# First seven node tiles of a graph layer made inside the edge stage, and the node stage begun at the eighth

## The chip, the cores and the metric

One core of one Trainium2 chip runs the whole kernel as one program. The metric is the device time of that core in microseconds (us). Its engines are TensorE (PE, with its weight loads as PEld), VectorE (DVE), ScalarE (ACT), GpSimd (POOL) and SyncE (SP). SP issues plain transfers. POOL issues the indirect ones, the gathers and scatters by a list of row numbers.

## What is computed

The reference is a graph attention layer over 6,250 nodes and 200,000 edges (sorted by destination), and after it a mixture of 8 experts with 2 chosen for each node. Cut to what matters:

```python
enh = LN(x) + 0.1 * query_emb
Q, K, V = enh @ Wq + bq, enh @ Wk + bk, enh @ Wv + bv        # 4 heads of 64
scores = einsum(Q[dst], K[src] + 0.2 * rel_w[edge_type]) / 8
w = softmax of scores over the edges of each dst
agg = segment_sum(w * V[src], dst)                            # V itself where a node has no edge
x1 = x + LN(agg @ Wo + bo + LN(x)) * gamma + beta
logits = LN-input x1 @ Wr + br; two best experts, softmax weights
out = x1 + sum over the two: weight * (gelu(LN_e(x1) @ W1[e] + b1[e]) @ W2[e] + b2[e])
```

(The router reads the normalized x1, as the experts do.)

## The kernel before

Three stages follow each other: `prepare` (K and V of all nodes to DRAM, index tables), `edge_pass` (attention over the edges) and `finish` (node tiles, routing and experts).

**Edge stage.** The edges are cut into 261 groups (`NG`), each of 6 x 128 edges (`TG`), half of them from each of two streams that run through the sorted list side by side. Every engine runs `pipeline(...)`: steps up to `WARM` = 8 are written out, the rest is a loop on the chip of 6 steps a round (`U` = `RING` = 6), and the last two or three steps are written out again. A step of group g does this. POOL issues six indirect gathers of K and V rows (line 260), ahead by the ring of six buffers: it waits until group g-6 has been summed (`s_agg`). PE turns the K half of group g+1 (L502), makes the scores of g in `psD` (L523, L525, L531), sums group g-1 (L555, L544) and turns the weights of g (L578). DVE takes the row maximum of `psD` (L426), ACT the exponential (L353). SP stores finished sums (L234) and loads edge features (L242) once in three groups. In the first eight groups PE also makes pieces of Q ("units", L488), which ACT evicts (L315). POOL computes `spots`, the row of the sums that belongs to each node, after its last gather (L276 to L291).

**Last stage.** `finish` goes through 72 steps written out in full. Of the 49 tiles of 128 nodes (`NT`) one begins in each step. For tile t: SP loads V and x rows (L1507, L1508), POOL gathers its sums (L1579), DVE divides them (L1802 to L1809), PE turns the messages and multiplies by Wo (L2072, L2084, L2086), DVE and ACT normalize twice (L1818 to L1841, L1648, L1734, L1719), SP stores x1 to `out` (L1545), PE makes the logits (L2102). Seven tiles (`RN`) are a batch. Batch k is routed in three steps: the two best experts are picked (16 DVE operations, `R_AT`), slots are counted (17, `S_AT`), and the list of expert blocks is made (23, `T_AT`). Then ACT scales the rows and POOL scatters them to `d_xs` (L1655, L1625), 14 scatters a batch. Expert blocks of 128 rows (105 of them) start at step `START` = 15; the first seven come one a step, the others two a step. The first needs batch 0 scattered and listed. Before `START` the steps hold node tiles alone. SP also loads the expert weights W2 in eight pieces of 1 MB (L1539), at steps 2, 4, 5, 7, 8, 10, 11 and 13, and the first three of W1, 1 MB each (L1514), at step 13. The router weights, gamma, beta and the router bias are loaded at the start of the stage (L1521 to L1525), and the first tile's normalization waits for all five.

`hold` is a wait on a semaphore ahead of a DMA, and stands in every queue as one instruction (L94). Each engine and SP is one queue in program order.

Of the kernel before, what the change touches and what calls it, by code (L numbers as in the profile page):

```python
# [17 lines left out]
P = 128  # L18
# [5 lines left out]
W = 16  # L24
# [20 lines left out]
SPOTS = NG * P // 4  # L45
# [22 lines left out]
def pipeline(eng, n, lo, hi, unroll, warm, step):  # L68
# [70 lines left out]

RING = 6  # L140
# [7 lines left out]
def edge_pass(nc, ctx, cst, idx, QT, kv_dram, idxall, feat_dram, accs_dram, bases, delta, penc, relT, reach, keys, spots, wq, bqc):  # L148
# [24 lines left out]
    place = sb("e_place", [P, 8, NT])  # L173
# [8 lines left out]
    psL = ctx.enter_context(nc.psum_tensor("psL", [P, DC, QH], F32))  # L182
    MX, MC, MM, NM, AL, SUM = (slice(i, i + 1) for i in range(6))
# [4 lines left out]
    s_idx = sem("es_idx")  # L188
    s_rows = [sem(f"es_rows{i}") for i in range(U // HB)]
# [34 lines left out]
    with nc.Block() as blk:  # L224
        @blk.sync
        def _(sp):
# [19 lines left out]
            pipeline(sp, NHB, 0, 3, U // HB, 5, step)  # L246
# [4 lines left out]
        def _(pool):  # L251
# [12 lines left out]
            pipeline(pool, NG, 0, 0, U, WARM, step)  # L264
# [8 lines left out]
            def spotted():  # L273
# [15 lines left out]
                link(pool.tensor_scalar(last, last, float(-P // 4 - SPOTS), None, ALU.add))  # L289
                link(pool.tensor_tensor(row, last, kept, ALU.mult))  # L290
                link(pool.tensor_scalar(spots[:, :], row, float(SPOTS), None, ALU.add))  # L291
# [4 lines left out]
        def _(act):  # L296
# [83 lines left out]
            pipeline(act, NG, -AHEAD, HI, U, WARM, step)  # L380

        @blk.vector
        def _(dve):
# [8 lines left out]
            dve.wait_ge(s_init, 4)  # L392

            def step(T):
# [61 lines left out]
                if isinstance(g.t, int):  # L456
                    tile = g.t if 0 <= g.t < SOON else None
                else:
                    tile = g.rnd + (SOON - WARM // U) if g.slot == WARM % U else None
                if tile is not None:  # L460
# [6 lines left out]
            pipeline(dve, NG, LO, HI, U, WARM, step)  # L467

        @blk.tensor
        def _(pe):  # L470
# [111 lines left out]
            pipeline(pe, NG, LO, HI, U, WARM, step)  # L582
# [22 lines left out]
def prepare(nc, ctx, cst, io, out, dram, idx, QT, idxall, bases, delta, penc, relT, unfit, reach, keys, wq, wo, bqc, consts,  # L605
# [42 lines left out]
    early = sb("p_early", [1, 4])  # L648
# [53 lines left out]
    with nc.Block() as blk:  # L702
# [40 lines left out]
        def _(pool):  # L743
# [76 lines left out]
            pool.dma_start(dram["accs"][NG * P:].rearrange("(p a) x -> p (a x)", a=2), zero[0:P // 4, 0:2 * ROW]  # L820
# [35 lines left out]
        def _(dve):  # L856
# [18 lines left out]
            def setup():  # L875
# [94 lines left out]
                link(dve.tensor_copy(early[:, 3:4], misfits[0:1, 1:2]))  # L970
                yield
# [339 lines left out]
START = RN + 8  # L1311
# [33 lines left out]
assert all(step_of(b) >= (batch_of(b) + 1) * RN + 8 for b in range(NB))  # L1345


def finish(nc, ctx, cst, io, out, dram, rows, ints, spots, wo, lnst, biaso):


    def sb(name, shape, dt=F32):
# [909 lines left out]
```

## Time and profile before

| what | us |
|---|---|
| median of 3 runs | 3764.64 (3761.67 to 3767.57) |
| the profiled execution, its own time | 3765.22 |
| its span from first to last instruction | 3763.4 |
| edge stage, first to last score maximum (L426) | 172.9 to 2718.6 |
| last stage, first instruction to first expert matmul (L2133) | 2727.3 to 2843.9 |

The profile is one execution. A PE record shows when a matmul was handed to the array; its end is modelled. "<-" names what ended an idle time, "remote" is an event that the profile ties to no instruction, "issue" an idle time with no visible cause. In the windows view each engine has its busy time and, in brackets, its number of instructions; PEclk is the granted TensorE clock as a share of full speed.

### The profile page before, as it was taken

To read this page: it belongs to the slowest core of one execution; us is meant where nothing else is said; L and a number is where in the kernel's file an instruction comes from. 1 tells how busy PE (TensorE), PEld (TensorE's weight loads), DVE (VectorE), ACT (ScalarE), POOL (GpSimd) and SP (SyncE) were. 2 spreads that over 40 slices of the span, in tenths; PEclk is the share of its full clock that TensorE was granted. 3 is DMA by queue.
4 is the path that set the end of the run, shared out by engine and by line. 5 is a ranking of instruction groups with operands and counts; after the bars stand their busy time and mean duration, and the time that the engine had idled before them with its cause. 6 is when DMAs were issued, how large, how long until landed. Compare 5 with 4: busy or idle time off the path is not lost. (4 is left out here: it accounts for less than half of the span.)

```text
span 3763.4 us, 77621 instructions
## 1 busy us (share of the span) xinstructions
PE 2924.2 (78%) x21213; PEld 2095.5 (56%) x21213; DVE 1675.9 (45%) x6070; ACT 1452.9 (39%) x4666; POOL 1904.0 (51%) x2003
## 2 busy tenths in 40 slices
PE   8687777777777777777777777777757999999998
PEld 7454444444444444444444444444446888889898
DVE  7244444444444444444444444444476554563222
ACT  5343333333333333333333333333335655564332
POOL 6355555555555555555555555555434434432322
PEclk9898888888888888888888888888858999999999
DMA  7566666666666666666666666666476666666665
GB/s 230 165 171 191 184 187 184 190 189 187 184 184 188 189 188 184 187 184 191 188 183 187 184 191 189 185 187 184 138 232 191 200 199 195 197 182 184 188 183 133
DMA packets 295467, 701.49 MB, mean 186 GB/s; under 512 B 47432, under 2 KB 143071, under 8 KB 295188
## 3 DMA queue, kind: packets, MB, share of 16 engines
q0 software_dynamic: 151104, 456.15, 43.5%
q1 hardware_dynamic: 144212, 243.57, 21.2%
q8 instruction: 65, 1.06, 0.1%
q14 instruction: 86, 0.70, 0.1%
HBM read 633.18 MB, written 66.36 MB: 186 GB/s over the span
## 5 line engine op out<-in xcount | busy, mean ns | idle before, releaser
L260 POOL DMA_INDIRECT e_kv<-d_kv,idx x1566 | 1486.4, 949 | 1140.2 <-PE psA L544 690.3
L426 DVE TENSOR_REDUCE e_small<-psD 128x1 f32<-128x384 f32 x261 | 145.5, 557 | 1255.8 <-remote 1250.6
L502 PE MATMUL psK<-consts,e_kv 128*128 128x128 f32 x3132 | 604.3, 316 | 90.8 <-issue 84.2
L353 ACT ACTIVATE e_prob<-psD,e_small 128x384 f32<-128x384 f32 x261 | 151.5, 580 | 1321.4 <-DVE e_small L432 1309.8
L544 PE MATMUL psA<-e_kv,e_probT 128*32 128x128 f32 x6264 | 441.2, 290 | 219.8 <-issue 218.6
L502 PEld LDWEIGHTS psK<-consts,e_kv 128*128 128x128 f32 x3132 | 432.2, 162 | 143.0 <-issue 137.9
L578 PE MATMUL psP<-consts,e_prob 128*128 128x128 f32 x783 | 177.2, 346 | 349.5 <-ACT e_prob L353 349.5
L1600 POOL DMA_INDIRECT out<-f_y,f_whose x105 | 165.8, 1579 | 554.1 <-DVE f_y L1978 387.8
L2146 PE MATMUL f_psY<-f_w,f_hT 128*128 x1680 | 395.1, 389 | 40.0 <-ACT f_hT L1668 34.0
L544 PEld LDWEIGHTS psA<-e_kv,e_probT 128*32 128x32 f32 x6264 | 181.3, 110 | 429.1 <-issue 401.6
L2133 PE MATMUL f_psH<-f_xT,f_w 128*128 128x128 f32 x3360 | 404.3, 280 | 0.9 <-DVE f_xT L1966 0.9
L1668 ACT ACTIVATE f_hT<-f_psH,f_b 128x128 f32<-128x128 f32 x840 | 239.0, 369 | 419.2 <-PE f_psH L2133 343.9
L2133 PEld LDWEIGHTS f_psH<-f_xT,f_w 128*128 128x128 f32 x3360 | 396.6, 196 | 3.6 <-issue 1.3
L2146 PEld LDWEIGHTS f_psY<-f_w,f_hT 128*128 128x128 f32 x1680 | 317.3, 194 | 85.4 <-issue 45.6
L332 ACT COPY e_qb<-QT 64x32 f32 x1044 | 229.2, 220 | 276.4 <-issue 257.3
L578 PEld LDWEIGHTS psP<-consts,e_prob 128*128 128x128 f32 x783 | 98.7, 166 | 421.9 <-ACT e_prob L353 420.2
L399 DVE COPY e_kT<-psK 128x384 f32<-128x384 f32 x522 | 289.9, 555 | 92.8 <-remote 35.5
L531 PE MATMUL psD<-e_kT,e_qb 128*32 128x384 f32 x2088 | 297.2, 651 | 0.0
L338 ACT COPY e_kT<-psK 128x384 f32<-128x384 f32 x522 | 246.4, 472 | 32.8 <-remote 13.9
L555 PEld LDWEIGHTS psA<-e_accs,e_carry 128*128 128x128 f32 x522 | 93.4, 224 | 226.8 <-issue 225.8
L1966 DVE TENSOR_SCALAR f_xT<-f_psT,f_ln 128x128 f32<-128x128 f32 x210 | 76.7, 406 | 292.0 <-PE f_psT L2123 218.2
L525 PE MATMUL psD<-e_relhot,e_qrel_high 128*128 128x384 f32 x261 | 172.2, 660 | 0.0
(309 smaller groups left out, 4108.3 us busy)
## 6 DMA issues: line engine op xcount, KB each, us to landing
f_w<-in_W SPq DMA_DIRECT2D x113, 1024.0 KB
e_rows<-d_feat SPq DMA_DIRECT2D x174, 288.0 KB
e_kv<-d_kv,idx POOLq DMA_INDIRECT x1566
d_accs<-e_accs SPq DMA_DIRECT2D x348, 48.8 KB
f_xs<-d_xs SPq DMA_DIRECT2D x105, 132.5 KB
d_kv<-p_kv SPq DMA_DIRECT2D x48, 256.0 KB, 2.1
p_x<-in_x SPq DMA_DIRECT2D x49, 128.0 KB, 2.8
n_v<-d_kv SPq DMA_DIRECT2D x49, 128.0 KB
```

Of the source, the lines that this page charges most:

```text
L260: pool.indirect_dma_start(out=kv[g.slot][:, t, :], out_offset=None, in_=kv_dram[:, :], in_offset=bass.IndirectOffsetOnAxis(ap=idx[g.slot][ ...
L332: act.copy(qb[a.slot % R][o * HD:(o + 1) * HD, :].rearrange("p (c b w o) -> p c b w o", c=2, b=DC, o=2)[:, c, :, :, o], QT[o * HD:(o + 1) ...
L338: act.copy(kT[a.slot % 2][:, 1, j * GH:(j + 1) * GH], psK[:, 1, 0:GH]).then_inc(s_kTa, 1)
L399: dve.tensor_copy(kT[a.slot % 2][:, 0, j * GH:(j + 1) * GH], psK[:, 0, 0:GH]).then_inc(s_kTv, 1)
L502: mm = pe.transpose(psK[:, half, t * P:(t + 1) * P], kv[a.slot][:, third * TS + t, half * P:(half + 1) * P], ident)
L525: pe.matmul(scores, part[:, :], relhot[g.slot % R][:, :], start=False, stop=False)
L531: mm = pe.matmul(psD[own, g.slot % 2, 0:GH], qb[g.slot % R][:, own], kT[g.slot % 2][:, b, c * GH:(c + 1) * GH], start=False, stop=True, ti ...
L544: mm = pe.matmul(psA[own, 0:2 * HD], probT[c.slot % R][:, j, own], kv[c.slot][:, s * TS + j, D + b * P:D + (b + 1) * P], start=j == 0, sto ...
L578: mm = pe.transpose(psP[:, j * P:(j + 1) * P], prob[g.slot % R][:, j * P:(j + 1) * P], ident)
L1668: act.activation(hT[:, f, :], psH[:, f // FB % 2, f % FB * BK:(f % FB + 1) * BK], ACT.Gelu, bias=b1[:, bass.ds(e * FC + f, 1)]).then_inc(s ...
L2133: mm = pe.matmul(psH[:, f // FB % 2, f % FB * BK:(f % FB + 1) * BK], w1[g % RW][:, a, f * P:(f + 1) * P], xT[g % 2][:, a, :], start=a == 0 ...
L2146: mm = pe.matmul(psY[:, 0:D], hT[:, f, :], w2[:, bass.ds(e * (FC * D) + f * D, D)], start=f == 0, stop=f == FC - 1)
```

## The change

Seven of the 49 tiles (`FORE` = 7) are made inside the edge stage, one in every nine groups (`PACE`) from group 192 on (`FOREAT`), each spread over 12 groups with one short piece for an engine in a group. For this the loop on the chip ends at `UNTIL` = 183 and steps 182 to 262 are written out on every engine. The gathers of the seven tiles read only sums stored before group 180 (`STORED`); a check of the data sends everything to the slow path when that isn't enough. The row numbers of the seven tiles are worked out on DVE in groups 184 to 191 (16 operations, two a group), and POOL waits for them ahead of its first such gather. The constants for the tiles are loaded by SP in the edge stage. The last stage then has 42 tiles (`NTF`), its `START` is 8, batch 0 is picked in step 0, placed in step 1 and listed in step 2. It fetches the seven stored x1 tiles back and normalizes them in step 0. W2 is loaded at steps 1, 3, 4, 6, 7, 8, 9 and 10, each but the first behind a hold for the piece before, and the first seven expert blocks wait only for their own expert's piece. W1's first three pieces go to steps 4, 5 and 6.

The constants, the end of the loop, and which tile has its piece in a step:

```diff
-START = RN + 8
+START = RN + 8 - FORE
...
+FORE = RN
+PACE, HOPS = 9, 11
+FOREAT = (NG - 4 - PACE * (FORE - 1) - HOPS) // HB * HB
+STORED = FOREAT - 4 * HB
...
+    if until is not None:
+        loops = min(loops, (until - warm) // unroll)
...
+def fore_of(step, hop):
+    if not isinstance(step, int):
+        return None
+    j, past = divmod(step - FOREAT - hop, PACE)
+    return j if past == 0 and 0 <= j < FORE else None
```

At the end of an engine's edge step the piece for its hop follows: PE `turn` at hop 2, `project` 3, `turn_again` 9, `route` 10; DVE `summed` 1, `normed` 4, `attended` 6, `factor` 8, `routed` 10; ACT `first_norm` 1, `copied` 2, `spread` 5, `spread_again` 7, `second_norm` 8, `copied_again` 9; POOL `gather` 1 behind its six gathers; SP `load` 6 and `store` 12 in its feature step, which runs some five groups ahead of PE. Hop 10 of a tile is hop 1 of the next. The pieces hold the same operations as a tile has in `finish`, on one set of buffers. POOL's piece, and the ones that the prediction prices:

```diff
+                j = fore_of(g.t, 1)
+                if j is not None:
+                    if j == 0:
+                        pool.wait_ge(s_soon, SITES)
+                        for i in range(U // HB):
+                            hold(pool, s_out[i], 2 * DC * 16 * len(range(i, STORED // HB, U // HB)))
+                    fore.gather(pool, j, accs_all[0:P // 2 + STORED * P], soon)
...
+    def load(self, sp, j):
+        if j + self.runs:
+            hold(sp, self.s_st, self.moved(j, 16))
+            hold(sp, self.s_act, self.shaped(j - 1, self.H2))
+        sp.dma_start(self.v, self.kv[j * P:(j + 1) * P, D:2 * D]).then_inc(self.s_in, 16)
+        sp.dma_start(self.x, self.io["x"][j * P:(j + 1) * P, :]).then_inc(self.s_in, 16)
...
+    def gather(self, pool, j, table, spots):
+        if j + self.runs:
+            hold(pool, self.s_row, self.row(j - 1, self.SUM))
+        pool.indirect_dma_start(
+            out=self.agg, out_offset=None, in_=table.rearrange("(q a) x -> q (a x)", a=4),
+            in_offset=bass.IndirectOffsetOnAxis(ap=spots[:, j:j + 1], axis=0)).then_inc(self.s_ag, 16)
...
+    def spread(self, act, j):
+        act.preload_act_table(ACT.Sqrt)
+        act.wait_ge(self.s_row, self.row(j, self.NORM))
+        act.activation(self.st[:, 8:9], self.st[:, 7:8], ACT.Sqrt, bias=self.cst("eps")).then_inc(self.s_act, 1)
+        act.preload_act_table(ACT.Exp)
...
+    def turn(self, pe, j):
+        pe.wait_ge(self.s_row, self.row(j, self.SUM))
+        if j + self.runs:
+            pe.wait_ge(self.s_act, self.shaped(j, 0))
+        for b in range(DC):
+            mm = pe.transpose(self.ps[:, b * P:(b + 1) * P], self.msg[:, b * P:(b + 1) * P], self.cst("ident"))
+        mm.then_inc(self.s_mm, 1)
+
+    def project(self, pe, j):
+        pe.wait_ge(self.s_act, self.shaped(j, self.TURNED))
+        to = self.ps[:, D:2 * D]
+        pe.matmul(to, self.cst("ones")[0:1, :], self.biaso[0:1, :], start=True, stop=False)
+        for b in range(DC):
+            mm = pe.matmul(to, self.turned[:, b, :], self.wo[:, b, :], start=False, stop=b == DC - 1)
+        mm.then_inc(self.s_mm, 1)
```

In `finish`:

```diff
-    W2_AT = {2 + (3 * e + 1) // 2: e for e in range(NX)}
+    W2_AT = {s: e for e, s in enumerate((1, 3, 4, 6, 7, 8, 9, 10))}
...
+    picked_at = lambda s: 0 if s == 0 else batch(s, R_AT)
+    placed_at = lambda s: 0 if s == 1 else batch(s, S_AT)
+    listed_at = lambda s: 0 if s == 2 else batch(s, T_AT)
...
-            for a in range(DC):
-                sp.dma_start(wr[:, a, :], io["Wr"][a * P:(a + 1) * P, :]).then_inc(s_w, 16)
-            for j, name in enumerate(("gamma", "beta")):
...
             load(2)
+            for j in range(FORE):
+                sp.dma_start(h2[j][:, :], out[j * P:(j + 1) * P, :]).then_inc(s_rows, 16)
             load(3)
...
+                    if e:
+                        hold(sp, s_w2, e * 16)
...
+                if s == 0:
+                    act.wait_ge(s_set, SETS)
+                    for j in range(FORE):
+                        act.wait_ge(s_rows, 16 * FORE)
+                        act.activation(h2[j][:, :], h2[j][:, :], ACT.Identity, bias=nb[:, j:j + 1], scale=rs[:, j:j + 1]
+                                       ).then_inc(s_fore, 1)
...
-                if c == 0:
+                if c < certain(0):
+                    pe.wait_ge(s_w2, (e + 1) * 16)
+                elif c == certain(0):
                     pe.wait_ge(s_w2, 16 * NX)
```

## Rows read from the trace of the kernel before

**Rows 1.** Windows: us, busy of PE, PEld, DVE, ACT, POOL, PEclk, DMA share, GB/s.

```profile
172.00:239.00 67.00, 60.32 (x423) 43.70 (x424) 32.92 (x105) 32.37 (x100) 28.69 (x30) 0.94 0.49 135
...
600.00:1600.00 1000.00, 728.17 (x5701) 446.48 (x5699) 426.17 (x1557) 343.26 (x1219) 578.70 (x611) 0.85 0.66 187
...
2703.00:2718.00 15.00, 15.00 (x162) 9.43 (x162) 10.77 (x43) 9.99 (x31) 0.84 (x3) 1.00 0.06 13
2727.00:2744.00 17.00, 7.14 (x18) 4.26 (x18) 9.02 (x32) 3.42 (x7) 8.92 (x13) 0.50 0.73 206
2744.00:2786.00 42.00, 29.73 (x100) 21.43 (x99) 35.64 (x129) 18.39 (x49) 11.46 (x18) 0.58 0.87 285
2786.00:2844.00 58.00, 25.74 (x85) 18.31 (x83) 36.44 (x154) 20.91 (x55) 22.87 (x27) 0.56 0.67 218
2844.00:2930.00 86.00, 73.35 (x448) 67.39 (x449) 60.45 (x209) 53.88 (x123) 35.74 (x38) 0.91 0.54 164
```

**Rows 2.** One line's instructions (L426, one a group) in three stretches.

```profile
L426 DVE TENSOR_REDUCE e_small<-psD x7: 548/558/558, 172.9 to 239.3; 128x1 f32<-128x384 f32 x7
L426 DVE TENSOR_REDUCE e_small<-psD x102: 556/557/559, 300.6 to 1293.7; 128x1 f32<-128x384 f32 x102
L426 DVE TENSOR_REDUCE e_small<-psD x4: 557/558/559, 2703.3 to 2718.6; 128x1 f32<-128x384 f32 x4
```

**Rows 3.** Waits, 1000 to 2000 us: total, times, longest.

```profile
DVE e_small L426 <- remote: 502.0, 101, 6.3
POOL e_kv L260 <- PE psA L544: 268.1, 102, 3.2
```

**Rows 4.** Timeline of one group late in the edge stage: start, us.

```profile
2670.67 0.94 POOL L260 DMA_INDIRECT e_kv<-d_kv,idx  x1 [2.65 <-PE psA L544]
...
2674.18 1.51 PE L531 MATMUL psD<-e_kT,e_qb 128*32 128x384 f32 x8
...
2676.92 0.95 POOL L260 DMA_INDIRECT e_kv<-d_kv,idx  x1 [0.30 <-issue]
...
2679.26 0.56 DVE L426 TENSOR_REDUCE e_small<-psD 128x1 f32<-128x384 f32 x1 [5.00 <-remote]
```

**Rows 5.** Timeline of an early group.

```profile
220.29 0.94 POOL L260 DMA_INDIRECT e_kv<-d_kv,idx  x1 [2.96 <-PE psA L544]
...
228.81 0.56 DVE L426 TENSOR_REDUCE e_small<-psD 128x1 f32<-128x384 f32 x1 [4.85 <-remote]
```

**Rows 6.** L488, the extra units of the first groups: ns min/median/max.

```profile
L488 PE MATMUL psL<-QT,wq x112: 377/379/747, 175.6 to 238.7; 128*128 128x256 f32 x112
```

**Rows 7.** L1822 (one a tile) in two stretches, and L2133 from its first.

```profile
L1822 DVE TENSOR_TENSOR n_xb<-n_x,n_vec x9: 424/426/427, 2743.7 to 2785.6; 128x256 f32<-128x256 f32 x9
L1822 DVE TENSOR_TENSOR n_xb<-n_x,n_vec x7: 424/424/426, 2785.6 to 2836.8; 128x256 f32<-128x256 f32 x7
L2133 PE MATMUL f_psH<-f_xT,f_w x234: 274/275/554, 2843.9 to 2930.0; 128*128 128x128 f32 x117
```

**Rows 8.** Timeline of the first tiles of the last stage.

```profile
2733.51 0.69 PE L2072 MATMUL n_psM<-consts,n_msg 128*128 128x128 f32 x2 [5.01 <-DVE n_msg L1809]
...
2734.98 2.08 PE L2086 MATMUL n_psO<-wo,n_turned 128*128 128x256 f32 x4
...
2741.02 0.42 DVE L1818 TENSOR_TENSOR n_y<-n_psO,n_xn 128x256 f32<-128x256 f32 x1 [4.40 <-DMA n_br<-in_br]
...
2751.10 1.03 PE L2102 MATMUL n_psL<-n_wr,n_turned 128*128 128x8 f32 x4
```

**Rows 9.** ScalarE's table loads and its norm of a tile.

```profile
L1638 ACT ACT_TABLE_LOAD  x85: 1283/1283/1283, 2727.4 to 3471.0; - x85
L1719 ACT ACTIVATE n_h<-n_x,n_nb,n_rs 128x256 f32<-128x256 f32 x8 | 4.8, 600 | 4.0 <-DVE n_nb L1841 4.0
```

**Rows 10.** Last queue listed from 300 to 2600 us; then 3500 to 3760 us.

```profile
q1 hardware_dynamic: 47424, 61.61, 10.0%
...
q8 instruction: 15, 0.25, 0.3%
```

More of the change, by code:

```diff
@@ new lines, in fore_of, with fore_again, _ @@
+def fore_of(step, hop):
[3 more added lines that the diff above has]
+    return j if past == 0 and 0 <= j < FORE else None
+def fore_again(nc, ctx, f, table, spots):
+    f.ps = ctx.enter_context(nc.psum_tensor("g_psF", [P, 512], F32))
+    f.runs = 1
+    tiles = range(FORE)
+    with nc.Block() as blk:
+        @blk.sync
+        def _(sp):
+            for j in tiles:
+                f.load(sp, j)
+                f.store(sp, j)
+            sp.wait_ge(f.s_st, f.moved(FORE, 16))
+        @blk.gpsimd
+        def _(pool):
+            for j in tiles:
+                f.gather(pool, j, table, spots)
+        @blk.vector
+        def _(dve):
+            for j in tiles:
+                f.summed(dve, j)
+                f.normed(dve, j)
+                f.attended(dve, j)
+                f.factor(dve, j)
+                f.routed(dve, j)
+        @blk.scalar
+        def _(act):
+            for j in tiles:
+                f.first_norm(act, j)
+                f.copied(act, j)
+                f.spread(act, j)
+                f.spread_again(act, j)
+                f.second_norm(act, j)
+                f.copied_again(act, j)
+        @blk.tensor
+        def _(pe):
+            for j in tiles:
+                f.turn(pe, j)
+                f.project(pe, j)
+                f.turn_again(pe, j)
+                f.route(pe, j)
@@ L245, in step @@
                                      ).then_inc(s_rows[g.slot], 16)
-            pipeline(sp, NHB, 0, 3, U // HB, 5, step)
+                if not isinstance(g.t, int):
+                    return
+                if g.t * HB == FOREAT:
+                    hold(sp, s_q, len(QCH) + len(LATER))
+                    for j, name in enumerate(("gamma", "beta")):
+                        sp.dma_start(kept.vec[:, j, :], io[name].rearrange("(a d) -> a d", a=1).to_broadcast([P, D])
+                                     ).then_inc(fore.s_in, 16)
+                    for a in range(DC):
+                        sp.dma_start(kept.wr[:, a, :], io["Wr"][a * P:(a + 1) * P, :]).then_inc(fore.s_in, 16)
+                    sp.dma_start(kept.br[:, :], io["br"].rearrange("(a d) -> a d", a=1).to_broadcast([P, NX])
+                                 ).then_inc(fore.s_in, 16)
+                done, new = fore_of(g.t * HB, 12), fore_of(g.t * HB, 6)
+                if done is not None:
+                    fore.store(sp, done)
+                if new is not None:
+                    fore.load(sp, new)
+            pipeline(sp, NHB, 0, 3, U // HB, 5, step, UNTIL // HB)
+            sp.wait_ge(fore.s_st, 16 * FORE)
             for i in range(U // HB):
@@ L1344, with finish @@
 LISTED = max(hi - lo for lo, hi in map(listed_by, range(NK)))
-assert all(step_of(b) >= (batch_of(b) + 1) * RN + 8 for b in range(NB))
-def finish(nc, ctx, cst, io, out, dram, rows, ints, spots, wo, lnst, biaso):
+NTF = NT - FORE
+assert all(step_of(b) >= (batch_of(b) + 1) * RN + 8 - FORE for b in range(NB))
+def finish(nc, ctx, cst, io, out, dram, rows, ints, spots, wo, lnst, biaso, kept):
     def sb(name, shape, dt=F32):
@@ L1360, in finish @@
     B, RL, RS, RX = RN, 6, 3, 4
+    wr, br, vec = kept.wr, kept.br, kept.vec
     RE, RW = 4, 3
@@ L2057, in turn @@
             def turn(s, m):
-                t, half = ((tile(s), msg), (tile(s - 2), h2))[m]
+                t, half, first = ((tile(s), msg, 0), (tile(s - 2), h2, FORE))[m]
                 if t is None:
```

386 lines of the change are left out of this document (308 added, 78 removed).

## The prediction

> **What bounds the kernel now.** I read the windows by stage first, then the period of the edge groups, the waits and one group's timeline, and last the opening of the last stage.
>
> In the windows the reader is to see that no engine is full in the edge stage: PE is busy 73% of the time, POOL 58%, and DMA engines 66% at 187 GB/s. The stretch from 2703 us on, where POOL no longer gathers, has PE busy all the time and almost no transfer [rows 1]. One instruction a group, L426, gives the period: (1293.7 - 300.6) / 101 = 9.83 us in the middle, (2718.6 - 2703.3) / 3 = 5.10 us once the gathers are over, and (239.3 - 172.9) / 6 = 11.07 us at the start, where the steps are written out and PE makes units of Q as well [rows 2]. So a group's compute needs 5.1 us, and something that goes with the gathers makes it 9.8.
>
> The waits name two: DVE waits 5.0 us in each group for an event that the profile doesn't name, POOL 2.6 us for PE's sums [rows 3]. The timeline joins them. POOL starts six gathers at 2670.67, one every 1.25 us, the last at 2676.92 and over at 2677.87. L531 is handed over at 2674.18, yet its maximum starts at 2679.26, 1.39 us after the last gather and 8.59 us after POOL's start [rows 4]. In an early group, with other work around it, the maximum again stands 8.52 us behind POOL's start [rows 5]. POOL then waits for the sums and starts 1.2 us after the maximum: 8.6 + 1.2 = 9.8. So I read the edge stage as a ring of POOL's burst of gathers and the end of a group's PE work, in which PE, DVE and ACT have some slack and POOL has none. The mechanism by which the burst holds PE's results back isn't in the profile; that it does is.
>
> The units are a measure of that slack: 112 records on PE in seven groups [rows 6].
>
> The last stage before its first expert matmul is a filling time: 2727.3 to 2843.9, 116.6 us with PE at half clock and half idle [rows 1, 7]. Nine tiles in a row go at (2785.6 - 2743.7) / 8 = 5.24 us each; the six intervals with batch 0 among them take (2836.8 - 2785.6) / 6 = 8.5 us [rows 7]. DMA moves 285 GB/s in the first of these stretches and 218 in the second [rows 1]. The first tile waits 4.40 us for the last of its constants [rows 8]. From the first expert block on PE paces the stage, in the same steps counted from `START` before and after.
>
> **The change, part by part.**
>
> *Removed: seven steps of filling.* `START` falls from 15 to 8. The three routing steps, the scatters and the first fetches stay, so what goes is seven steps that hold a tile alone: 7 x 5.24 = 36.7 us [rows 7]. Bounds: were some of the routing work to have no tile to overlap, as in step 0, the gain is less by no more than that work; ACT's part there is the seven norms of the stored rows, 7 x 0.60 = 4.2 us, and it stands in ACT ahead of the first tile's square root [rows 9]. The wait of 4.40 us for the constants goes [rows 8], and seven row loads stand on SP in place of five small ones. These two nearly cancel: +1 us.
>
> *Transfers in the filling time.* Before, 17 x 0.206 + 42 x 0.285 + 58 x 0.218 = 28.1 MB in it [rows 1]. After, seven tiles' gather, two loads and store (0.65 MB each) go, three of W2's pieces (3 MB) fall behind step 8, and 0.9 MB of stored rows come: 28.1 - 4.6 - 3.0 + 0.9 = 21.4 MB. At the 241 GB/s of the whole filling time that is 89 us, at the 285 GB/s of its best stretch 75. The steps alone give 116.6 - 36.7 + 1 = 81. SP's new holds between W2's pieces stand in front of its tile loads, x1 stores and W1 loads, so a late piece is passed on to them; I take 83 us, with 76 and 92 as bounds. Gain 33.6.
>
> *W2's last three pieces* fall beside the first expert blocks, where DMA moves 164 GB/s [rows 1]; 3 MB over three blocks lift that under 285. W1 for the next block shares the queues. I take 1 us, at most 4.
>
> *Added in the edge stage: POOL.* One gather more in seven of the groups, 7 x 1.25 = 8.8 us if the ring is as I read it [rows 4]; 0 if it fits in POOL's wait of 2.6 us [rows 3]. Since the maximum kept its distance from the burst in two quite different groups, I take 8.8.
>
> The Trainium skill speaks against that price: by its page "SBUF — State Buffer", section "SBUF: two separate sides", engine ports and DMA ports are apart and neither a transfer nor a compute operation slows the other. By that rule the extra gather would be free, and the forecast lower by 8.8 us. The halving of the period when the gathers end says that here something of the burst does reach PE [rows 2].
>
> *Added: PE.* At half clock a tile is two turns of 0.69 us, the product by Wo of 2.08 us, its one-row bias matmul at about half of that, 1.04, and the logits' 1.03: 5.5 us over four groups, 39 us for seven tiles [rows 8]. It stands behind L578, ahead of the next group's turns. The units of the first groups price such work: PE was busy 60.32 / 67 x 11.07 = 10.0 us a group there against 0.73 x 9.83 = 7.2 in the middle, 2.8 more, and the period was 1.24 longer, 0.44 us for each us [rows 1, 2]. All of 39 us at that rate is 17 us; at full clock half; and as no group gets more than 3.1 us and most none, the slack between L531 and the maximum (5.1 us) may hide all. I take 6, with 0 and 17.
>
> *Added: ACT and DVE.* Two of ACT's pieces load two tables each, 2 x 1.28 us [rows 9], before ACT's copies for the next group; DVE's are under 2 us. Behind DVE's piece wait the next group's K copy and masks. Both engines stand idle some 5 us in a group [rows 3], and every piece waits for one made a group or more earlier, but for SP's loads of V and x, which run only about when `summed` wants them. 0, at most 3 for all. The feature loads behind them on SP come three groups ahead: 0.
>
> *POOL's wait before tile 0.* POOL is five groups ahead and stops in its step 193 until DVE has ended group 191, and its six gathers for 194 stand behind it. Meanwhile the groups run at 5.1 us instead of 9.8: two of them give 9 us back; then PE waits for a burst (7.2 us) with POOL's lead used up. I take 0, with -9 and +9.
>
> *Steps written out.* 79 more steps are fetched as new code. Between 300 and 2600 us the profile lists no instruction queue at all; in the written-out expert blocks it lists 15 packets of 16 KB in 260 us [rows 10], and those blocks keep their even pace. 0.
>
> The Trainium skill agrees: "Runtime: NRT & Kernel Launch", section "Instruction fetch mechanics", has straight code fetched ahead and mostly hidden, and a taken branch as what can stall.
>
> *Sum.* -36.7 + 1 + 2.1 (transfers) + 1 (W2) + 8.8 + 6 = -17.8 us. The profiled execution took 3765.2, so 3747.4; it stands 0.6 over the median of the runs, so 3747.
>
> **The rivals.**
>
> *The edge work is all hidden* (17%). POOL's wait takes the gather, as the rule above has it, and PE's slack the rest: 3764.6 - 32.6 = 3732. For it: idle time on every engine. Against: the constant 8.5 to 8.6 us.
>
> *Written-out steps are slower* (11%), the other sign. If the 1.24 us that the first groups cost over the middle [rows 2] came from fetching new code and not from the units, 79 steps cost 98 us: 3845. It decides from 17.8 / 79 = 0.23 us a step. Against it: the units are there to explain those groups, and the blocks of the last stage [rows 10].
>
> *The filling time is bound by transfers* (12%). At 241 GB/s or below, with SP blocked behind W2's holds, the first expert matmul comes after 92 us and later tiles' loads are late too: 9 us are lost of the gain and the edge work is paid at its upper price, 17 instead of 6: 3767, no change.
>
> *POOL's wait shifts the ring* (5%). With POOL's lead gone it would issue back to back, 7.5 us a group, and if the groups can follow, the 68 left gain 2.3 us each. Some 3600 to 3700.
>
> **How the numbers follow.** The forecast has 55%, with a range of its own of 3737 to 3759. 0.2% is 7.5 us, about what a measurement of this kernel tells from no change. Faster by more is most of the forecast (50), the hidden case (17), the shifted ring (5) and a part of the third (3): 75%. Within: 5 + 8 = 13%. Slower: 11 + 1 = 12%. For 8 in 10 the range goes from 3722 to 3768.
>
> **What would show it.** From the last stage's first instruction to the first L2133: 83 us. Groups 192 to 256: 9.83 us, and about two more in each group with a seventh gather; the maximum about 9.8 us behind POOL's start in those and 8.6 in the others. Groups 190 and 191 at about 5 us, and a wait on PE before 193's turns. The stretch from the first L2133 to the end within 3 us of before (919.5 us). The prediction is wrong if written-out groups without a piece differ from 9.83 us, if seventh gathers leave the period alone, or if the filling time isn't within 76 to 92 us.

## The result, and the profile after

The changed kernel takes 3730.62 us (median of 4 runs, 3730.37 to 3738.62) against 3763.15 for the kernel before (4 runs): ratio 0.9914, 95% interval 0.9901 to 0.9928, so 32.5 us less. The forecast was 3747, 16 us too high. The direction held, and so did the wide range (3722 to 3768); the forecast's own range (3737 to 3759) was missed. Three terms had the wrong size, and two of them nearly cancel.

The profiled execution has a span of 3728.8 us against 3763.4. The lines below are first the windows of the changed kernel's last stage before and around its first expert block (columns as in [rows 1]).

```profile
2733.00:2749.00 16.00, 6.65 (x17) 4.04 (x18) 12.16 (x51) 4.61 (x9) 8.12 (x11) 0.50 0.83 253
2749.00:2807.00 58.00, 26.84 (x91) 19.10 (x89) 39.12 (x155) 25.03 (x65) 26.86 (x32) 0.56 0.82 276
2807.00:2893.00 86.00, 72.65 (x433) 65.91 (x432) 58.84 (x207) 53.82 (x122) 36.25 (x38) 0.90 0.66 205
```

The same single lines as before, now of the changed kernel: L766 is the maximum of a group (L426 before), L212 the early tiles' gather, L2014 the table load that opens the last stage (L1638 before), L2210 one a tile (L1822 before), L2521 the expert matmul (L2133 before).

```profile
L766 DVE TENSOR_REDUCE e_small<-psD x68: 541/557/559, 2087.1 to 2724.1; 128x1 f32<-128x384 f32 x68
...
L212 POOL DMA_INDIRECT fore_work<-d_accs,e_soon x7: 945/949/1043, 2051.6 to 2575.2; - x7
...
L2014 ACT ACT_TABLE_LOAD  x85: 1283/1283/1283, 2733.0 to 3437.6; - x85
...
L2210 DVE TENSOR_TENSOR n_xb<-n_x,wq x8: 424/425/426, 2749.1 to 2805.2; 128x256 f32<-128x256 f32 x8
...
L2521 PE MATMUL f_psH<-f_xT,f_w x3360: 272/275/550, 2807.2 to 3714.5; 128*128 128x128 f32 x198
```

Of the kernel before, the maxima of groups 193 to 260:

```profile
L426 DVE TENSOR_REDUCE e_small<-psD x68: 556/558/559, 2081.2 to 2718.6; 128x1 f32<-128x384 f32 x68
```

The reader is to see where the 34.6 us of span went. The last group's maximum starts at 2724.1 instead of 2718.6 [rows 2]: the edge stage is 5.5 us longer (forecast: 8.8 + 6 = 14.8). From the table load to the first expert matmul it is 2807.2 - 2733.0 = 74.2 us; before, 2843.9 - 2727.4 = 116.5 [rows 7, 9]: 42.3 us less (forecast: 33.6). From there to the end 921.6 instead of 919.5 us, 2.1 more (forecast: 1). 5.5 - 42.3 + 2.1 = -34.7, and 0.1 between the stages.

Groups 193 to 260 take 2724.1 - 2087.1 = 637.0 us with seven tiles among them, and 2718.6 - 2081.2 = 637.4 before. That looks like free work. The timeline of the changed kernel around the first early tile shows that it isn't.

```profile
2033.99 0.94 POOL L536 DMA_INDIRECT e_kv<-d_kv,idx  x1 [0.31 <-issue]
...
2046.82 0.56 DVE L766 TENSOR_REDUCE e_small<-psD 128x1 f32<-128x384 f32 x1
...
2050.52 0.17 DVE L728 TENSOR_SCALAR e_soon<-e_site 128x7 int32<-128x7 f32 x1
...
2051.59 1.04 POOL L212 DMA_INDIRECT fore_work<-d_accs,e_soon  x1 [16.65 <-DVE e_soon L728]
2052.09 0.56 DVE L766 TENSOR_REDUCE e_small<-psD 128x1 f32<-128x384 f32 x1
2052.93 0.95 POOL L536 DMA_INDIRECT e_kv<-d_kv,idx  x1 [0.30 <-issue]
...
2063.05 1.54 PE L861 MATMUL psK<-consts,e_kv 128*128 128x128 f32 x6 [7.84 <-DMA e_kv<-d_kv,idx]
...
2081.76 0.94 POOL L536 DMA_INDIRECT e_kv<-d_kv,idx  x1 [0.30 <-issue]
...
2087.13 0.56 DVE L766 TENSOR_REDUCE e_small<-psD 128x1 f32<-128x384 f32 x1 [9.00 <-remote]
```

POOL stands for 16.65 us behind L728, the last of the steps that work out the early tiles' indices. Meanwhile the groups run faster, the last two at 6.5 and 5.3 us (the maxima stand at 2040.27, 2046.82 and 2052.09), near the 5 us of the forecast, until POOL's lead is gone. Then POOL issues the 24 gathers of four groups without a break, from 2052.93 to 2082.7, and from one maximum to the next 35.0 us pass. So the pause did cost. Something else must have paid for it.

### The profile page after: what moved, and what is told of

The parts are those of the page before. It is cut to its first block and busy times, and to the rows that moved or that the text cites. A ratio compares the mean times of both kernels' runs of the same rounds, so it can differ in the third digit from the quotient of the medians.

```text
span 3728.8 us, 75315 instructions
## 1 busy us (share of the span) xinstructions
PE 2926.8 (78%) x21220; PEld 2065.2 (55%) x21220; DVE 1685.9 (45%) x6098; ACT 1501.4 (40%) x4701; POOL 1910.4 (51%) x1996
## 5 line engine op out<-in xcount | busy, mean ns | idle before, releaser
L536 POOL DMA_INDIRECT e_kv<-d_kv,idx x1566 | 1494.0, 954 | 1112.3 <-PE psA L903 503.8
L861 PEld LDWEIGHTS psK<-consts,e_kv 128*128 128x128 f32 x3132 | 423.6, 162 | 259.4 <-issue 198.4
L766 DVE TENSOR_REDUCE e_small<-psD 128x1 f32<-128x384 f32 x261 | 145.3, 557 | 886.4 <-remote 815.3
L2536 PE MATMUL f_psY<-f_w,f_hT 128*128 x1680 | 396.4, 389 | 39.9 <-ACT f_hT L2044 32.5
L2521 PE MATMUL f_psH<-f_xT,f_w 128*128 128x128 f32 x3360 | 402.6, 279 | 0.0
L2521 PEld LDWEIGHTS f_psH<-f_xT,f_w 128*128 128x128 f32 x3360 | 395.1, 195 | 2.7 <-issue 0.3
L903 PEld LDWEIGHTS psA<-e_kv,e_probT 128*32 128x32 f32 x6264 | 167.9, 111 | 368.2 <-issue 341.6
L2356 DVE TENSOR_SCALAR f_xT<-f_psT,f_ln 128x128 f32<-128x128 f32 x210 | 76.8, 406 | 290.6 <-PE f_psT L2511 219.7
L923 PE MATMUL psX<-e_qb,relT 128*128 128x128 f32 x522 | 134.7, 342 | 62.9 <-issue 28.1
```

Source lines behind the costliest of these rows:

```text
L536: pool.indirect_dma_start(out=kv[g.slot][:, t, :], out_offset=None, in_=kv_dram[:, :], in_offset=bass.IndirectOffsetOnAxis(ap=idx[g.slot][ ...
L861: mm = pe.transpose(psK[:, half, t * P:(t + 1) * P], kv[a.slot][:, third * TS + t, half * P:(half + 1) * P], ident)
L903: mm = pe.matmul(psA[own, 0:2 * HD], probT[c.slot % R][:, j, own], kv[c.slot][:, s * TS + j, D + b * P:D + (b + 1) * P], start=j == 0, sto ...
L2521: mm = pe.matmul(psH[:, f // FB % 2, f % FB * BK:(f % FB + 1) * BK], w1[g % RW][:, a, f * P:(f + 1) * P], xT[g % 2][:, a, :], start=a == 0 ...
L2536: mm = pe.matmul(psY[:, 0:D], hT[:, f, :], w2[:, bass.ds(e * (FC * D) + f * D, D)], start=f == 0, stop=f == FC - 1)
```

## The experiments

**Two kinds of chips.** The runs x1 to x18 stood on seven chips. On three (x9 to x11, x16 and x18, as on the chip of the result) the kernel before takes 3764 to 3808 us; on four (x1 to x8, x12 to x15, x17) it takes 3093 to 3101 us. I call them the first and the second kind. Every ratio below is against runs of the kernel before on the same chip.

**Written-out steps alone: x1, x12, x16.** The kernel before with

```
-    loops = max((n + lo - warm) // unroll ...)
+    loops = min(the same, (183 - warm) // unroll)      # in all five edge pipelines
```

> The kernel before with only one thing of the change: its five edge pipelines leave their loops at step 182, and the last 79 steps are written out. Theory A (the two traces: the groups around 180 run at 7.5 to 8.3 us once the loop ends, and POOL's lead falls by one): about 9 us gained at the switch and nothing lost afterwards, 3754 against 3763. The prediction on record put it at 0: 3763. The rival on record, written-out steps cost 1.24 us each: 3845 or more. A gain in every written-out group would show as a period under 9.83 us all the way to group 256.

> The same kernel as x1. On a chip of the first kind (kernel before at 3763): theory A, written-out groups run at 9.6 us instead of 9.83, 79 x 0.2 = 16 us faster, 3747, ratio 0.9957; prediction on record: 0, 3763. On a chip of the second kind: no difference, as in x1.

> The same kernel as x1 and x12. On a chip of the first kind: theory A, written-out groups run at 9.6 us instead of 9.83, 79 x 0.2 = 16 us faster, 3747, ratio 0.9957; prediction on record: 0, 3763. On a chip of the second kind: no difference.

On the second kind: 0.9996 (0.9987 to 1.0005) and 0.9997 (0.9988 to 1.0006), no difference beyond 0.13%. On the first kind, x16: 3749.06 against 3764.7 us, ratio 0.9960 (0.9946 to 0.9974), 15.6 us. Its line of the maximum (L428 there), in the loop and behind it:

```profile
L428 DVE TENSOR_REDUCE e_small<-psD x95: 557/558/559, 1027.5 to 1951.8; 128x1 f32<-128x384 f32 x95
...
L428 DVE TENSOR_REDUCE e_small<-psD x68: 541/557/560, 2072.9 to 2700.9; 128x1 f32<-128x384 f32 x68
```

In the loop 924.3 / 94 = 9.83 us a group. Written out, groups 193 to 260 take 628.0 us, 9.4 less than before, and group 193 comes at 2072.9, 8.3 earlier: 17.7 us in all beside that trace. Beside x9, which is the kernel before on another chip of the first kind, the same two numbers are 11.1 and 3.9, 15.0 us in all. Theory A of the expectations (written-out groups are shorter) stands for this kind, and the prediction's 0 for these steps falls.

**The whole edge stage written out: x2, x13.** As x1, with no loop at all.

> The kernel before with no loop in the edge stage at all: every step of its five pipelines is written out, from the first. If the gain of written-out steps comes once, where a loop is left, it is not there or stays at 9 us: 3754 to 3763. If it comes with each written-out step (0.12 us, 9 us over 79 steps), 174 more steps give 21 us on top: some 3733. If fetching new code costs anything (rival on record, 1.24 us a step), it is over 3900. The trace is to show the period of groups 30 to 180 beside 9.83.

> The same kernel as x2. On a chip of the first kind: theory A, 253 written-out groups at 0.2 us less each, some 50 us faster, 3713; if only leaving the loop gives something, as x12. On a chip of the second kind: no difference.

Both met the second kind: 0.9999 (0.9990 to 1.0008) and 0.9995 (0.9986 to 1.0004). What they do show is that fetching 253 steps as new code costs nothing that can be measured there, and what a loop adds. The heads of the pages of x1 and x2:

```profile
span 3090.8 us, 75262 instructions
```

```profile
span 3094.9 us, 69922 instructions
```

5340 fewer instructions for 174 steps, 31 a step, with the same products and copies. By the kinds of instruction in the two traces, 2899 register additions (ALU_OP), 3116 fused register operations, 342 moves and loads of a base and 144 branches are gone, and 1161 plain semaphore waits have come.

**The pause: x3, x15.** The changed kernel, with the indices worked out eight groups earlier:

```
-    UNTIL = FOREAT - 9
+    UNTIL = FOREAT - 18
-                if isinstance(g.t, int) and FOREAT - 8 <= g.t < FOREAT:
+                if isinstance(g.t, int) and FOREAT - 16 <= g.t < FOREAT - 8:
                     next(sites)
```

> The changed kernel with the indices of the seven gathers worked out eight groups earlier (in groups 176 to 183), so that POOL doesn't wait for them; the edge steps are written out from 170 instead of 182. Theory A: POOL's pause cost a gap of 35 us at group 193 against some 19 us given back before it, so without it the ring keeps its lead and the time falls by about 15 us, to 3716. Prediction on record: the pause is worth 0, with -9 to +9: 3722 to 3740. The maximum of group 193 should start at about 2072 us instead of 2087.

> The same kernel as x3. First kind of chip: theory A, the pause costs 16 us net (a gap of 35 us less what the groups before it gain), so 3715, ratio 0.9872; prediction on record: pause at 0, no difference to x14. Second kind of chip: 5 to 7 us under x14, 3066.

Second kind both: 0.9905 (0.9889 to 0.9920) and 0.9907 (0.9892 to 0.9923). The same edit on the first kind is in x10 below. The changed kernel beside it:

**The changed kernel again: x5, x14.**

> The changed kernel as it is, beside the kernel before on this chip. The four runs before this one stood on a chip where the kernel before takes 3097 us instead of 3763, with a period of 7.5 us in the edge stage (POOL's six gathers one behind the other) in place of 9.8. If the change is worth the same on both, the ratio is 0.991 again, as on the first chip (0.9914). If POOL's pause before tile 0 and the extra gathers cost more where POOL never waits (7 x 1.25 = 8.8 us for the gathers and up to 15 for the pause), the ratio is 0.993 or more there.

> The changed kernel, for comparison in the same call. First kind of chip: 3731 beside 3763, ratio 0.9914; second kind: 0.993.

0.9929 (0.9915 to 0.9943) and 0.9921 (0.9907 to 0.9934). So the change is worth nearly as much there, though its parts are other ones. On the same chip x15 was 3.9 us under x14, where 5 to 7 were expected. Group 193's maximum starts at 1612.9 in x14 and 1602.1 in x15. The intervals of x14 and x15 overlap; the traces, not the times, carry this price on the second kind.

**One gather of seven: x4.** The changed kernel with

```
     def gather(self, pool, j, table, spots):
-        if j + self.runs:
-            hold(pool, self.s_row, self.row(j - 1, self.SUM))
+        if j:
+            return
```

> The changed kernel with six of the seven extra gathers left out: all seven tiles take the rows that the first one gathered, so the output of tiles 1 to 6 is not the reference's, and all other work stays. Prediction on record: each gather costs the ring 1.25 us, so this saves 7.5 us: 3723. Rival (they fit into POOL's own wait, as the averages over nine groups of 9.47 to 9.95 us suggest): 0 to 2 us, 3729 to 3731.

Ratio 0.9891 (0.9876 to 0.9907), against 0.9929 and 0.9921 of the changed kernel on two other chips: 9 to 12 us less, where 7.5 were expected. The line of the maximum, groups 193 to 260, of x1 (kernel before but for the loop), x5 (changed) and x4:

```profile
L428 DVE TENSOR_REDUCE e_small<-psD x68: 540/557/559, 1601.4 to 2104.1; 128x1 f32<-128x384 f32 x68
```

```profile
L766 DVE TENSOR_REDUCE e_small<-psD x68: 540/557/559, 1609.5 to 2119.6; 128x1 f32<-128x384 f32 x68
```

```profile
L766 DVE TENSOR_REDUCE e_small<-psD x68: 540/557/559, 1614.4 to 2118.2; 128x1 f32<-128x384 f32 x68
```

502.7, 510.1 and 503.8 us. 502.7 / 67 = 7.50 us is six gathers of 1.25: on this kind POOL sets the pace. The first of the seven extra gathers stands ahead of group 193 (at 1594.0 in x5), so this stretch has six of them. Six should add 7.5 us there, and 7.4 were added with all the tiles' work; six fewer took 6.3 off. The tiles' other work adds about 1 us (503.8 less 502.7).

**PE's pieces twice: x6.** The changed kernel with each turn and product of the early tiles made twice; in `turn`, and alike in the three others:

```
-        for b in range(DC):
+        for b in (*range(DC), *range(DC)):
             mm = pe.transpose(...)
```

> The changed kernel with every product and turn of the seven early tiles made twice on PE (39 us more PE work at half clock, the output is the same). Prediction on record: the PE pieces cost 6 us, 17 at most, so the same again: 3737, at most 3748 where the changed kernel takes 3731. Rival (all of it is hidden in PE's slack): within 2 us of the changed kernel.

0.9927 (0.9914 to 0.9939) beside x5's 0.9929 on the same chip; groups 193 to 260 take 2121.9 - 1610.7 = 511.2 us, 1.1 more than in x5. On the second kind PE's pieces are hidden. On the first kind this was not run.

**One step more, and no holds: x7, x8.**

```
-START = RN + 8 - FORE
+START = RN + 9 - FORE          # x7
-                    if e:
-                        hold(sp, s_w2, e * 16)          # x8
```

> The changed kernel with the first expert block one step later (step 9 of the last stage instead of 8). Prediction on record: a filling step that holds a tile alone is worth 5.24 us, so +5.2 us. Rival from comparing the traces (the filling time fell by 42.4 us over seven steps, 6.1 a step): +6 or more. If the filling time is bound by something else than steps (transfers, the batch's list), less than 3 us.

> The changed kernel without SP's holds between the pieces of W2 (each piece waits for the one before it to land in the changed kernel). Prediction on record: the holds make the tile loads late and cost up to 2 us of the filling time: 0 to 2 us faster. Rival: they keep W2 from crowding out the tiles' transfers, and without them the filling time is 3 to 8 us longer.

0.9938 (0.9925 to 0.9951) and 0.9918 (0.9905 to 0.9930), beside 0.9929: neither can be told from x5 by its time. For x7 the trace tells more. Table load and expert matmul of x5, then of x7:

```profile
L2014 ACT ACT_TABLE_LOAD  x85: 1283/1283/1283, 2128.4 to 2792.1; - x85
...
L2521 PE MATMUL f_psH<-f_xT,f_w x3360: 272/275/553, 2198.8 to 3057.9; 128*128 128x128 f32 x198
```

```profile
L2014 ACT ACT_TABLE_LOAD  x83: 1283/1283/1283, 2126.7 to 2776.8; - x83
...
L2521 PE MATMUL f_psH<-f_xT,f_w x3360: 272/275/552, 2203.5 to 3057.3; 128*128 128x128 f32 x198
```

The filling time is 70.4 us in x5 and 76.8 in x7: the step costs 6.4 us, nearer the rival than the prediction's 5.24. From the first to the last expert matmul x5 takes 859.1 us and x7 853.8, so some of the 6.4 us may come back; but x14, the same kernel as x5, takes 856.0, so most of that difference is scatter between executions. In x8 the filling time is 1.2 us shorter than in x5 (by its own lines 2193.3 - 2124.1 = 69.2). That can't be told from scatter either: x15, which has the holds, takes 69.3, and x17, which hasn't, 70.1. On the first kind it is 76.4 in x10 without holds, 75.8 in x11 and 74.2 in the changed kernel with them. The rival of 3 to 8 us more falls on the second kind; no gain of leaving the holds out is shown on either.

**The first kind again: x9, x10, x11.** x9 is the kernel before. x10 is x3 and x8 in one, x11 is x3 and x4 in one.

> The kernel before as it is, for its trace on the chip of this call, where its period in the edge stage is 7.5 us (POOL's six gathers one behind the other) or 9.8 us (the first chip). Time as the kernel before in the same call. Between the last group's maximum and the first expert matmul it should take 121 to 125 us, against 79 in the changed kernel, on either.

> The changed kernel with both: the indices eight groups earlier (x3) and no holds between W2's pieces (x8). If each gives what its trace showed on its own (the edge stage 5 us shorter by the pause, the filling time 1 us by the holds) it is 0.2% under the changed kernel: 3066 where that takes 3072, ratio 0.991. If the pause cost nothing and x3's and x8's lower medians were scatter: 3072, 0.993.

> The indices eight groups earlier, and only the first of the seven extra gathers made (the output of tiles 1 to 6 is not the reference's). Where POOL's gathers set the pace, six fewer are 6 x 1.25 = 7.5 us (prediction's price of a gather), so 7 us under x3 and x10: some 3060, and groups 193 to 260 should take 502 us as before instead of 510. Rival: the price of a gather is nothing, and the 8 us of that stretch come from the tiles' other work: no difference to x10.

x9 takes 3762.2 us, and from the last group's maximum to the first expert matmul 2841.5 - 2715.9 = 125.6 us, as expected; its filling time is 116.8. In the changed kernel on this kind the same stretch is 83.1 us, not the 79 of the second kind. x10 takes 3713.83 us against 3764.15, ratio 0.9869 (0.9852 to 0.9885); x11 3711.59, ratio 0.9859 (0.9842 to 0.9875). The expectations had been written for the second kind, and x10's ratio is lower than they said. Its interval and the changed kernel's (0.9901 to 0.9928) don't overlap: on this kind the earlier indices, with twelve more steps written out and no holds, are worth 0.45%, some 17 us. The line of the maximum, groups 193 to 260, of x9, x10 and x11:

```profile
L426 DVE TENSOR_REDUCE e_small<-psD x68: 557/558/559, 2076.8 to 2715.9; 128x1 f32<-128x384 f32 x68
```

```profile
L766 DVE TENSOR_REDUCE e_small<-psD x68: 539/557/559, 2066.7 to 2708.5; 128x1 f32<-128x384 f32 x68
```

```profile
L766 DVE TENSOR_REDUCE e_small<-psD x68: 541/557/560, 2061.3 to 2693.2; 128x1 f32<-128x384 f32 x68
```

Without the pause group 193 comes at 2066.7 and 2061.3 instead of 2087.1. Groups 193 to 260 take 641.8 us in x10 and 631.9 in x11: six gathers are worth 9.9 us here by these two, and x10's stretch against x16's (641.8 - 628.0) gives 13.8 for all that the tiles add, where the changed kernel gives 9.0. The two timed medians, 2 us apart with overlapping intervals, don't show that difference; x11's profiled execution was its fastest by 12 us. So on the first kind a gather is worth 9.9 / 6 = 1.65 us by these traces and (3713.83 - 3711.59) / 6 = 0.4 by the medians; the runs don't settle it.

**All together: x17, x18.** x10 with the whole edge stage written out (`UNTIL = 8`).

> x10 (indices earlier, no holds) with the whole edge stage written out, no loop in it. First kind of chip (kernel before at 3763): if each written-out step gives 0.2 us, some 35 us under x10's 3714: 3680, ratio 0.978, and groups 30 to 180 at 9.6 us; if the gain is tied to leaving the loop at 182: 3714, groups 30 to 180 at 9.83. Second kind: as x15, 3066, ratio 0.991.

> The same kernel as x17. First kind of chip (kernel before at 3763): if each written-out step gives 0.2 us, some 35 us under x10's 3714: 3680, ratio 0.978, and groups 30 to 180 at 9.6 us; if the gain is tied to leaving the loop at 182: 3714, ratio 0.987. Second kind: as x17, ratio 0.988.

x17, second kind: 3063.95 against 3100.74 us, ratio 0.9882 (0.9866 to 0.9899). x18, first kind, on a chip where the kernel before takes 3807.51 us: 3703.95, ratio 0.9730 (0.9716 to 0.9745), where 3680 and 0.978 were expected. It beats the kernel before and the changed kernel on both kinds. Its maxima from group 32 to 176, all in what had been the loop:

```profile
L766 DVE TENSOR_REDUCE e_small<-psD x145: 541/558/559, 490.1 to 1883.9; 128x1 f32<-128x384 f32 x145
```

1393.8 / 144 = 9.68 us, against 9.83 in the loops of the kernel before and 9.79 in x10's own loop (groups 30 to 170). So the gain appears in written-out steps wherever they stand, by 0.10 to 0.15 us a step here; the 9.6 that was expected isn't reached. There is no trace of the kernel before on that chip, which is slower by 43 us for it, so part of the ratio may be the chip's own: x18's time is only 10 us under x10's.

## Why the prediction was right and wrong

The terms below come from single traces on different chips of the first kind, and these scatter. Up to group 170 all of them run the same loop, yet its maximum starts at 1854.4 us in the kernel before, 1853.8 in x16, 1851.4 in x9, 1849.2 in the changed kernel, 1845.9 in x10 and 1843.0 in x11. Lengths of stretches are steadier than starting times:

| us | before | x9 (before) | x16 | changed | x10 | x11 |
|---|---|---|---|---|---|---|
| groups 181 to 193 | 118.4 | 117.5 | 111.2 | 130.9 | 117.4 | 116.6 |
| groups 193 to 260 | 637.4 | 639.1 | 628.0 | 637.0 | 641.8 | 631.9 |
| filling (table load to first expert matmul) | 116.5 | 116.8 | 117.9 | 74.2 | 76.4 | 75.8 |
| first expert matmul to the end | 919.5 | 918.9 | 922.9 | 921.6 | 916.5 | 918.9 |

The lines of the first row for the kernel before, x16, the changed kernel and x10:

```profile
L426 DVE TENSOR_REDUCE e_small<-psD x13: 557/558/558, 1962.8 to 2081.2; 128x1 f32<-128x384 f32 x13
```

```profile
L428 DVE TENSOR_REDUCE e_small<-psD x13: 542/558/558, 1961.7 to 2072.9; 128x1 f32<-128x384 f32 x13
```

```profile
L766 DVE TENSOR_REDUCE e_small<-psD x13: 541/558/558, 1956.2 to 2087.1; 128x1 f32<-128x384 f32 x13
```

```profile
L766 DVE TENSOR_REDUCE e_small<-psD x13: 542/557/559, 1949.3 to 2066.7; 128x1 f32<-128x384 f32 x13
```

*The steps written out: 0 forecast, -17.7 us measured* (x16 beside the kernel before; 15.0 beside x9, 15.6 by the times). This is the first step that failed. The prediction asked what new code costs to fetch, and had that right: nothing that shows (x2, x13; the instruction queues of [rows 10] were read rightly). The rival of 98 us more is excluded. It never asked what leaving the loop removes: 31 instructions a step, register arithmetic and branches. That a written-out group is shorter on the first kind is shown. That those instructions are the reason is an inference, and which of them is open; on the second kind the same ones go and nothing is gained. The Trainium skill ("Runtime: NRT & Kernel Launch", section "Instruction fetch mechanics") gives as one reason for unrolling that a taken branch to code not yet fetched breaks the prefetch. The direction agrees with x16 (0.9960) and not with x1 and x12 (0.9996 and 0.9997), and no trace here shows a stall at the branch.

*POOL's wait before tile 0: 0 forecast with -9 to +9, +14.2 us measured* (group 193 at 2087.1 in the changed kernel, 2072.9 in x16). Part of that is scatter ahead of the pause. By groups 181 to 193 the pause costs 19.7 us beside x16 and 13.5 and 14.3 beside x10 and x11, so 13 to 20. This is the second failed step, outside its bounds by any of these. The first half of the mechanism was right: two groups at 6.5 and 5.3 us, the lead used up. The second half, "then PE waits for a burst (7.2 us)", priced one burst. After the pause POOL owed four, and in the stretch in which it issued them one behind the other the groups stood for 35 us. x10 and x11, which have no pause, begin group 193 20 and 26 us before the changed kernel; 7 and 12 us of that lie ahead of group 181 (scatter, and some of the twelve more steps that they have written out). On the second kind group 193 comes 10.8 us earlier without the pause in x15 beside x14, and 6.4 in x3 beside x5. There POOL waits only 9.4 us in x14 and 3.9 in x5, and while it then issues gather after gather the groups go on: the interval before group 193 is 11.0 us in x5. On both kinds the pause costs about what POOL waits.

*The extra gathers and PE's pieces: 8.8 + 6 = 14.8 forecast; 9.0 measured* on the first kind (637.0 in the changed kernel less 628.0 in x16; 13.8 with x10 in its place), 7.4 on the second (x5 less x1). As in x4, six of the seven gathers lie in that stretch. Right in kind, a little high. On the second kind the split is clear: the gathers cost nearly their full price (x4), the pieces nothing that shows (x6); the prediction's 6 us for PE were too many there. The average over groups alone, 637.0 against 637.4, would have called all of it free, and it took x16 to see that faster steps had paid. The ground for the price did fail on the first kind. The prediction took it from the 8.6 us between POOL's start and the maximum, and named the same distance in the new groups as a sign. It holds in the loop (8.6 us in x16, groups 100 to 169), but in the written-out groups 196 to 249 it is 4.2 us in x16 and 4.2 in the changed kernel, with the maximum mostly behind the third or fourth gather.

*The rule on SBUF.* By the traces of the second kind no contention is needed to price a gather: POOL issues one every 1.25 us and has no time to spare. The rule of the Trainium skill's "SBUF — State Buffer", section "SBUF: two separate sides", that transfers and compute operations don't slow each other isn't contradicted there. Yet the extra gather isn't free either, because POOL's own issue is the bound; the prediction's step from the rule to "free" left that out. On the first kind what holds the results back stays open (below).

*Seven steps of filling: -36.7 + 1 + 2.1 = -33.6 forecast, -42.3 us measured.* This is the third failed step, too small by 8.7 (by 6.8 if x9 and x10 are compared, 116.8 less 76.4). Before, eight intervals of 5.24 us run from the first L1822 to the ninth, and from there to the first expert matmul it is 2843.9 - 2785.6 = 58.3 us [rows 7]. In the changed kernel it is 58.1 us from the *first* L2210 (2749.1) to the first expert matmul (2807.2). So the stretch that batch 0's routing shares with the tiles is as long as it was, and eight lone intervals, 41.9 us, are gone. The prediction had counted seven steps. Batch 0's routing began in step 9 of 15 and now begins in step 0 of 8: nine steps that held a tile alone are gone, and two more lie under the routing, which takes no longer for them. The time before the first tile stayed (16.3 us before, 16.1 after, from the table load): the wait of 4.40 us for the constants [rows 8] went, and batch 0's routing, which DVE makes from step 0 on, took its place. The rival in which transfers hold the first block back to 92 us falls: it comes at 74.2 us, under the lower bound of 76, with 16 x 0.253 + 58 x 0.276 = 20.1 MB moved. Whether transfers have begun to bind isn't shown: 276 GB/s is near the 285 of the best stretch before, at which 20.1 MB take 70 us.

*W2's last pieces and what follows the first block: +1 forecast, +2.1 measured.* The last row of the table runs from 916.5 to 922.9 us, so neither number can be told from 0.

*The sum.* -17.8 forecast. The terms as measured: -17.7 (written out) + 14.2 (pause) + 9.0 (gathers and pieces) - 42.3 (filling) + 2.1 = -34.7. That this adds up is no proof of the parts, since starting times were subtracted in a chain. By the lengths from group 181 on, the edge stage's terms are -7.2 - 9.4 (written out) + 19.7 (pause) + 9.0 = +12.1, and the last maximum comes only 5.5 later because the changed kernel's trace was already 6.6 us ahead at group 181, in the loop, for which no term of the change is known. The hidden case's 3732 came near the result for another reason than its own: the edge work wasn't hidden.

*Left open.* Why the two kinds of chips differ by 18%. The instructions last the same (a gather 0.95 us, a maximum 0.56); PE's product lasts 1.51 us in one row and 0.85 in the other, but both lengths occur on both kinds, by the granted clock of the moment (0.84 and 0.88 in the mean from 1000 to 1500 us). The timeline of one group of x1, on the second kind, beside [rows 4]:

```profile
906.93 0.94 POOL L262 DMA_INDIRECT e_kv<-d_kv,idx  x1 [0.30 <-issue]
...
907.80 0.85 PE L535 MATMUL psD<-e_kT,e_qb 128*32 128x384 f32 x8
908.18 0.99 POOL L262 DMA_INDIRECT e_kv<-d_kv,idx  x1 [0.30 <-issue]
...
908.72 0.56 DVE L428 TENSOR_REDUCE e_small<-psD 128x1 f32<-128x384 f32 x1 [0.31 <-PE psD L535]
```

The maximum follows the product within 0.1 us, in the middle of POOL's burst. On the first kind, in the loop, it came 3.57 us after the product's end (2679.26 against 2674.18 + 1.51) and behind the burst, with "remote" as its releaser [rows 3, 4]. In x1's waits from 700 to 1450 us "remote" doesn't appear:

```profile
PE psK L506 <- DMA e_kv<-d_kv,idx: 143.6, 43, 6.2
...
DVE e_small L428 <- PE psD L535: 72.0, 83, 1.9
```

What that unnamed event is, no run here tells. The prediction's ring describes the loop on the first kind and nothing else. In this written-out group of x10 the maximum starts within the burst, 3.5 us behind POOL's start, and from burst to burst it is 9.5 us all the same. What sets that period isn't shown.

```profile
2052.72 0.94 POOL L536 DMA_INDIRECT e_kv<-d_kv,idx  x1 [2.37 <-remote]
...
2056.26 0.56 DVE L766 TENSOR_REDUCE e_small<-psD 128x1 f32<-128x384 f32 x1 [1.21 <-PE psD L890]
...
2062.26 0.94 POOL L536 DMA_INDIRECT e_kv<-d_kv,idx  x1 [2.34 <-remote]
```

## What to carry to other kernels

Where a change turns looped steps into written-out ones, price what the loop's own instructions may cost, not only the code that must be fetched (here 15 us on one kind of chip, nothing on the other); then price the added work against written-out steps without it, since averages over both hide each other. A pause of the engine that runs ahead can cost about as much as it lasts, though the other engines run on meanwhile (13 to 20 us for a wait of 16.65 on the first kind, 10.8 for 9.4 in x14), so what it waits for should be ready before its turn, which here is a matter of eight groups in one line. A single trace prices a stretch to a few us at best; compare lengths from a point that the change leaves alone, and repeat the kernel before. When steps of a filling time are removed, count the intervals that stand alone in the trace before and after, since the shared part keeps its length.

## What the runs showed of the hardware

- The same kernel takes 3764 to 3808 us on some chips and 3093 to 3101 on others, with equal durations of the single gather and maximum; the period of the edge groups is 9.83 and 7.50 us. The ratio of this change was nearly the same on both (0.9914; 0.9929 and 0.9921), though its terms were not.
- 79 written-out steps gave 15.6 us of 3765 on the first kind (x16) and nothing beyond 0.13% on the second (x1, x12).
- On the first kind 24 gathers issued back to back (2052.93 to 2082.70) went with 35.0 us between two maxima. On the second kind gathers are issued back to back all along, and the maxima go on at 7.5 us a group (x1, x5).
- On the first kind a group takes 5.3 us while POOL stands still (2052.09 - 2046.82 in the changed kernel) and 5.1 after the last gather [rows 2]; what makes it 9.83 goes with the gathers.
